# Row maxima of the two widest query blocks: half copied by ScalarE, a VectorE scan over both halves, the causal mask by TensorE, and a new order

## The reference, cut to what matters

```python
x = layernorm(inputs); qkv = (x @ W_qkv + b).reshape(4, 16, 1024, 48)
q, k, v = split(qkv); qk = einsum('bhse,bhte->bhst', q, k) * 512 ** -0.5
attn = softmax(qk + triu(-inf, k=1)); sa = attn @ v; out = sa @ W_out + b_out
# light_ffn(x) and scatter(heavy_ffn(x[top 256 by routing])) are added
```

## Time and profile before

| | |
|---|---|
| time, median of 3 runs (lowest to highest) | 708.96 us (708.54 to 710.82) |
| span of the profiled execution (first to last instruction) | 705.6 us |
| own time of the profiled execution | not listed apart from its span; the median is 3.4 us above the span |
| busy: PE, DVE, ACT, POOL | 660.3, 563.1, 392.4, 380.6 us |
| mean granted TensorE clock | 0.979 |

### The profile page before, as it was taken

How to read it: one execution, slowest core, us unless ns; L and a number is a source line. 1 busy time by engine, 2 the same in 40 slices (tenths; PEclk the granted TensorE clock), 3 DMA queues, 4 the chain that set the end, 5 groups by cost and what they waited for, 6 DMA issues and landing times. The chain is left out here.

```text
span 705.6 us, 12334 instructions
## 1 busy us (share of the span) xinstructions
PE 660.3 (94%) x3923; PEld 291.7 (41%) x3923; DVE 563.1 (80%) x1587; ACT 392.4 (56%) x876; POOL 380.6 (54%) x774
## 2 busy tenths in 40 slices
PE   4995999899999999989999999999999999999995
PEld 2552555333333333323323333333333434678675
DVE  4853888899999999999999999999999595563211
ACT  2331322387877777728858868777776565230210
POOL 4663550358858657657886755554543274431603
PEclk9997999899999999979999999999999999999999
DMA  8675999769786676795999648458484261956512
GB/s 274 195 183 159 230 237 235 173 134 153 136 140 138 90 139 103 97 145 94 164 152 150 122 87 120 74 54 118 79 159 35 42 123 34 207 107 163 106 60 30
DMA packets 259776, 92.48 MB, mean 131 GB/s; under 512 B 229808, under 2 KB 245328, under 8 KB 256592
## 3 DMA queue, kind: packets, MB, share of 16 engines
q1 hardware_dynamic: 258176, 89.60, 65.9%
q0 software_dynamic: 1536, 2.10, 1.7%
HBM read 56.65 MB, written 35.01 MB: 130 GB/s over the span
## 5 line engine op out<-in xcount | busy, mean ns | idle before, releaser
L1268 DVE CUSTOM_DVE_ANT_0 ps<-ps,maskrow 128x640 f32<-128x640 f32 (+7 forms) x512 | 375.3, 779 | 27.6 <-PE ps L1034 26.0
L904 ACT ACTIVATE strips<-ps 128x512 f32<-128x512 f32 (+1 forms) x608 | 313.0, 577 | 111.0 <-PE ps L1076 88.7
L1034 PE MATMUL ps<-QTk,QTq 96*128 96x512 bf16 (+3 forms) x768 | 190.5, 337 | 22.6 <-DVE mx L1268 15.4
L1076 PE MATMUL ps<-QTq,QTk 99*128 99x512 bf16 (+3 forms) x768 | 185.4, 331 | 1.5 <-DMA QTq<-m_d 0.6
L1094 PE MATMUL ps<-strips,vext 128*32 128x512 f32 (+3 forms) x1536 | 162.0, 497 | 0.9 <-DVE oT L1291 0.4
L1034 PEld LDWEIGHTS ps<-QTk,QTq 96*128 96x128 bf16 x768 | 53.7, 98 | 170.9 <-DVE mx L1268 137.2
L1076 PEld LDWEIGHTS ps<-QTq,QTk 99*128 99x128 bf16 x768 | 68.4, 98 | 88.3 <-ACT strips L904 40.2
L1747 POOL TENSOR_SCALAR_AFFINE_SELECT strips<-strips 128x512 f32<-128x512 f32 x128 | 79.4, 636 | 41.6 <-ACT strips L904 41.2
L994 PE MATMUL ps<-shared,xrT 128*128 128x384 f32 (+1 forms) x256 | 94.9, 503 | 0.1
L1268 DVE DVE_READ_ACCUMULATOR2_ANT mx<- 128x1 f32 x512 | 72.3, 141 | 0.0
L1640 POOL TENSOR_TENSOR r<-qkT,pieces 128x1024 f32<-128x1024 f32 x16 | 34.1, 2132 | 50.2 <-ACT pieces L883 41.9
(11 more groups left out here) (154 smaller groups left out, 668.3 us busy)
## 6 DMA issues: line engine op xcount, KB each, us to landing
pieces_d<-pieces SPq DMA_DIRECT2D x64, 192.0 KB, 3.5
qk<-qkv_d SPq DMA_DIRECT2D x64, 128.0 KB, 3.9
qkv_d<-shared SPq DMA_DIRECT2D x16, 384.0 KB, 4.0
QTq<-pieces_d SPq DMA_DIRECT2D x16, 384.0 KB, 5.1
QTk<-pieces_d SPq DMA_DIRECT2D x16, 384.0 KB, 7.6
QTq<-pieces_d SPq DMA_DIRECT2D x16, 256.0 KB, 5.7
QTk<-pieces_d SPq DMA_DIRECT2D x16, 256.0 KB, 8.3
vext<-qkv_d SPq DMA_DIRECT2D x16, 256.0 KB, 5.8
```

What stands on the lines that cost most here:

```text
L904: nc.scalar.activation(dst, src, ACT.Exp, scale=SCALE).then_inc(exp_done, 1)
L1034: mm = pe.matmul(psM[:, s, at:at + n], QTq[0:W, f % 3, c * 1024 + qb * P:c * 1024 + (qb + 1) * P], QTk[0:W, f % 3, c * 1024 + k0:c * 1024 ...
L1076: mm = pe.matmul(psE[:, (NE * q + j) % ES, k * n:(k + 1) * n], QTk[0:W + 3, q % 3, c * 1024 + kb * P:c * 1024 + (kb + 1) * P], QTq[0:W + 3 ...
L1268: ins = nc.vector.tensor_tensor_reduce(scores, scores, maskrow[:, 1024 - n:1024], 1.0, MASKED, ALU.add, ALU.max, mx[:, f % 2, 8 * c + qb:8 ...
```

## The change

Query blocks 7 and 6 (1024 and 896 scores a row) become "paired" items, in steps 2 to 15. For each of them TensorE computes the products as before and then adds the causal mask in PSUM by one more 128 x 128 product (`eye` times `barred`). ScalarE copies the left half of the scores to SBUF (`half_copied`, items "H"; two buffers, laid over `xr` and `osb`). VectorE takes `tensor_tensor_scan` with max and max over the right half in PSUM and the copy in SBUF: element i of its output is the larger of output i-1, right[i] and left[i]. It writes 512 or 448 running maxima to `scan`, placed so that the last lands in the column of `mx` for that block. Since a scan overwrites what lies left of that column, the C items run from head 3 down to head 0, with the narrow blocks of a head behind the scans (`maxima_of`), and each item waits for the scan before it. `mx` is now one buffer and part of `scan`. The blocks 0 to 5 are handled as before.

```diff
-UNITS = ((4,), (5,), (6,), (7,), (0, 1), (2, 3))
+UNITS = ((7,), (6,), (5,), (4,), (2, 3), (0, 1))
+PAIRED = (0, 1)
+def maxima_of(f):
+    return [("C", f) + x for c in range(3, -2, -1) for x in ((c, 0), (c + 1, 4), (c, 1), (c + 1, 5), (c, 2), (c, 3))
+            if 0 <= x[0] < 4]
+NHB = 2
-STEP, PACE = 29.60, 29.94
-SOON, LATER, BEHIND = 0.15, 8.0, 1.44
+STEP, PACE = 23.944, 24.244
+SOON, LATER, BEHIND = 0.150, 11.860, 1.729
...
+            if kind == "H":
+                n = HALVES.index(x) - NHB
+                return latest(after(("Tensor", ("C",) + x[1:])), after(("Vector", ("C",) + HALVES[n][1:] if n >= 0 else ("SMAX",))))
...
-            return ... if engine == "Tensor" else 0.12 + 0.00084 * n
+            return ... if engine == "Tensor" else 0.075 + 0.00082 * n
+        if kind == "H":
+            return 0.075 + 0.00082 * (UNITS[x[3]][0] + 1) * P / 2
+            if x[3] in PAIRED and x[1] > 1:
+                return product_time(widths[0]) + BARRED if engine == "Tensor" else 0.117 + widths[0] / 2 / 960
...
+            def half_copied(f, c, u):
+                s, at = place["C", f, c, u]
+                act.wait_ge(full[s], at + 1)
+                k, n = paired["C", f, c, u], (UNITS[u][0] + 1) * P // 2
+                if k == 1:
+                    act.wait_ge(smax_done, 1)
+                elif k >= NHB:
+                    so, to = place[("C",) + HALVES[k - NHB][1:]]
+                    act.wait_ge(free[so], to + 1)
+                nc.scalar.activation(half[k % NHB][:, 0:n], psM[:, s, 0:n], ACT.Copy).then_inc(half_done, 1)
...
+                            masked = item in paired and k0 + n == (qb + 1) * P
...
+                            if masked:
+                                mm = pe.matmul(psM[:, s, at - P:at], eye[:, :], barred[:, :], start=False, stop=True)
...
+                before = scan_before["C", f, c, u]
+                if before:
+                    so, to = place[before]
+                    dve.wait_ge(free[so], to + 1)
...
+                    if ("C", f, c, u) in paired:
+                        k = paired["C", f, c, u]
+                        dve.wait_ge(half_done, k + 1)
+                        scores = psM[:, s, n // 2:n]
+                        end = MXAT + 8 * c + qb + 1
+                        ins = nc.vector.tensor_tensor_scan(scan[:, end - n // 2:end], scores, half[k % NHB][:, 0:n // 2],
+                                                           MASKED, ALU.max, ALU.max)
+                        continue
```

More of the change, by code:

```diff
@@ L73 @@
 EARLY, BEGUN = 3, 12
-FIRST = [("C", f, c, u) for f in range(2) for c in range(4) for u in range(NU)][:4 * NU + BEGUN]
+def maxima_of(f):
+    return [("C", f) + x for c in range(3, -2, -1) for x in ((c, 0), (c + 1, 4), (c, 1), (c + 1, 5), (c, 2), (c, 3))
+            if 0 <= x[0] < 4]
+FIRST = (maxima_of(0) + maxima_of(1))[:4 * NU + BEGUN]
 NL = 8
+HALVES = [("H",) + x[1:] for x in [x for f in range(1, STEPS) for x in maxima_of(f)][BEGUN:]
+          if x[1] > 1 and x[3] in PAIRED]
+NHB = 2
+MXAT = 504
 LAG = 0.2
-STEP, PACE = 29.60, 29.94
-SOON, LATER, BEHIND = 0.15, 8.0, 1.44
+STEP, PACE = 23.944, 24.244
+SOON, LATER, BEHIND = 0.150, 11.860, 1.729
 OB = 1
@@ L89 @@
 LANDS = 1.6
+BARRED = 0.06
 def product_time(n):
@@ L103, in schedule @@
     chains = {
-        ("Tensor", "C"): [("C", f, c, u) for f in range(1, STEPS) for c in range(4) for u in range(NU)][BEGUN:],
+        ("Tensor", "C"): [x for f in range(1, STEPS) for x in maxima_of(f)][BEGUN:],
         ("Tensor", "E"): [("E", q, j) for q in range(STEPS) for j in range(NE)],
@@ L111, in schedule @@
         ("Scalar", "E"): [("E", q, j) for q in range(STEPS) for j in range(NE)],
+        ("Scalar", "H"): list(HALVES),
         ("Scalar", "R"): [x for r in range(N_ITERS) for x in (("RX", r), ("R", r))],
         ("Vector", "TP"): [("TP", f) for f in range(EARLY, STEPS)],
-        ("Vector", "C"): [("C", f, c, u) for f in range(1, STEPS) for c in range(4) for u in range(NU)][BEGUN:],
+        ("Vector", "C"): [x for f in range(1, STEPS) for x in maxima_of(f)][BEGUN:],
         ("Vector", "MXT"): [("MXT", f) for f in range(1, STEPS)],
@@ L191, in ready @@
             if kind == "KEY":
-                return latest(done.get(("landed", ("NA_IN",))), after(("Vector", ("C", STEPS - 1, 3, NU - 1))))
+                return latest(done.get(("landed", ("NA_IN",))), after(("Vector", ("C", STEPS - 1, 0, NU - 1))))
             if kind == "SMAX":
@@ L197, in ready @@
             if kind == "MXT":
-                return latest(after(("Vector", ("C", x[1], 3, NU - 1))), after(("Pool", ("MAX", x[1] - 1))) if x[1] > 1 else 0.0)
+                return latest(after(("Vector", ("C", x[1], 0, NU - 1))), after(("Pool", ("MAX", x[1] - 1))) if x[1] > 1 else 0.0)
             if kind == "OT":
@@ L207, in ready @@
                 return latest(after(("Pool", ("S", x[1] - 1) if x[1] else ("ROUTES",))), PACE * (0.9 + 0.75 * x[1]))
+            if kind == "C" and x[1] > 2 and x == maxima_of(x[1])[0]:
+                return after(("Scalar", ("H",) + x[1:]), ("Vector", ("MXT", x[1] - 1)))
+            if kind == "C" and x[3] in PAIRED and x[1] > 1:
+                return after(("Scalar", ("H",) + x[1:]))
             return after(("Tensor", x))
         if engine == "Scalar":
+            if kind == "H":
+                n = HALVES.index(x) - NHB
+                return latest(after(("Tensor", ("C",) + x[1:])), after(("Vector", ("C",) + HALVES[n][1:] if n >= 0 else ("SMAX",))))
             if kind == "P1":
@@ L273, in due @@
         if kind == "TP":
-            return STEP * (x[1] - 2.40)
+            return STEP * (x[1] - 2.388)
         if kind == "P1":
-            return STEP * (x[1] - 2.23)
-        if kind == "C":
-            return STEP * (x[1] - 1.61 + (NU * x[2] + x[3]) / (4 * NU))
+            return STEP * (x[1] - 2.218)
+        if kind in ("C", "H"):
+            return STEP * (x[1] - 1.756 + maxima_of(x[1]).index(("C",) + x[1:]) / (4 * NU))
         if kind == "E":
@@ L281, in due @@
         if kind == "PV":
-            return STEP * (x[1] + 0.38 + EXPS_OF[x[2:]] / NE)
+            return STEP * (x[1] + 0.366 + EXPS_OF[x[2:]] / NE)
         if kind == "CAUSAL":
@@ L285, in due @@
         if kind == "SPLIT":
-            return STEP * (x[1] - 2.31)
+            return STEP * (x[1] - 2.298)
         if kind in ("STORE", "LOAD", "LQK"):
-            return STEP * (x[1] - 2.13)
+            return STEP * (x[1] - 2.118)
         if kind == "BULK":
@@ L370, in layer_kernel @@
     order, slots, _ = schedule()
+    paired = {("C",) + x[1:]: n for n, x in enumerate(HALVES)}
     place = {x: (0, n) for n, x in enumerate(FIRST)}
@@ L376, in layer_kernel @@
         place[x] = n % MS, held[n % MS] + n // MS
+    scan_before, last_scan = {}, None
+    for x in [x for f in range(STEPS) for x in maxima_of(f)]:
+        scan_before[x] = last_scan
+        if x in paired:
+            last_scan = x
     ST = 10
@@ L472, in layer_kernel @@
         pmo = sb("pmo", [P, 2, 32, D])
-        mx = sb("mx", [P, 2, 32])
+        scan = sb("scan", [P, MXAT + 32])
+        mx = scan[:, MXAT:MXAT + 32]
+        sT = scan[0:NT, 0:P]
         mxT = sb("mxT", [P, 32])
@@ L520, in layer_kernel @@
                 oT[:, :, :, :].rearrange("p b n w -> p (b n w)")[:, 0:QKV]]
+        half = [xr[:, :, :].rearrange("p u e -> p (u e)"), osb[:, 0:512]]
         xs = strips[:, 0:NT * E].rearrange("p (t e) -> p t e", e=E)
@@ L1024, in ring_item @@
                     _, f, c, u = item
-                    if c == 0 and u == 0:
+                    if c == 3 and u == 0:
                         pe.wait_ge(qk_in[f % 3], 16 * 2 * len(RUNS) * (f // 3 + 1))
@@ L1106, in _ @@
                     project(t // 2, t % 2, h)
+            pe.wait_ge(consts, N_CONST)
             pe.wait_ge(qkv_done, NT)
@@ L1258, in largest @@
                 dve.wait_ge(full[s], at + 1)
-                if c == 0 and u == 0 and f >= 2:
-                    dve.wait_ge(mxt_done, f - 1)
+                if c == 3 and u == 0 and f >= 1:
+                    dve.wait_ge(mxt_done, f)
+                before = scan_before["C", f, c, u]
+                if before:
+                    so, to = place[before]
+                    dve.wait_ge(free[so], to + 1)
                 where = 0
```

30 lines of the change are left out of this document (19 added, 11 removed).

## The result

The changed kernel takes 763.4 us (median of 4 runs, 763.0 to 764.3) against 708.8 us; the ratio is 1.077 with a 95% interval of 1.074 to 1.079. The forecast was 758 us, with 700 to 790 as its range. The profiled execution has a span of 761.8 us.

The account below looks back on a forecast made before the run. VectorE was taken to bound the kernel at 29.5 us a step; a slot round of 33.0 us a step over 14 steps adds 49 us to 705.6, plus 3.4 from span to median: 758 us, range 700 to 790.

Parts of the forecast that it names:

- VectorE bounds the kernel before: From 140 to 555 us VectorE, 96% busy, was taken to set the pace, with 28.3 of 29.5 us a step.
- The mask product: On TensorE, 128 more columns for each paired item: 0.06 us, eight times a step, 0.5 us, in time TensorE has.
- The scan's price: On VectorE, 1.19 us for a scan of 512 and 1.05 for 448, so 9.0 us replace 8.8 a step.
- upper end: The scan at 2.08 ns an element, from GpSimd's subtraction, saving VectorE nothing; the lower end, at the maximum's rate, saves 4.0 us a step.
- The copies: On ScalarE, 0.60 and 0.55 us each, 4.6 us a step; ScalarE at 26.5 of 29.5 us still fits.
- The round of the slot: TensorE writes, ScalarE copies, VectorE reads one slot: 6.70 us of parts plus 1.56 of waits, 8.26 us a head.
- The sum: Steps 2 to 15 at 33.0 us instead of 29.5 add 49 us; 754.6 us of span, 758 us median.
- Rival 1: Scan at the maximum's rate, slot still sets the pace: 28.9 us a step, 701 us (687 to 717); chance 0.13.
- Rival 2: Quick scan, planner's order hides the rounds, ScalarE bounds at 26.5 us a step: 667 us; chance 0.05.
- Rival 3: Slow scan, copy hidden behind the other slot and VectorE's other duties: 29.7 us a step, 712 us; chance 0.13.
- Rival 4: Forecast with a mismatched order, in-order queues waiting for each other, TensorE's clock possibly lost: 785 us and above; chance 0.07.
- Front and tail unchanged: The parts before and after the steps with scans keep their time; the median stands 3.4 us above the span.

## Why the prediction was right, and where it wasn't

- *VectorE bounds the kernel before.* Only half true. VectorE is 96% busy, but TensorE is 97% busy in the same stretch (402.6 of 415 us). With 4 us a step of VectorE's work gone the kernel won 8 us, and 17 with a new plan, and TensorE was busy 386 of 390 us then. My sentence that TensorE "has this time" took its 119.9 us of waits for room. The mask product came out small all the same (3.6 us between the medians), so that this error cost the forecast little.
- *The scan's price.* Forecast 1.19 and 1.05 us from start to next start. Measured: 483.83 to 484.97 us, 1.14, and 485.58 to 486.56, 0.98. The median durations, 1223 and 1090 ns, are 64 elements apart: 2.08 ns an element.

```profile
L1333 DVE TENSOR_TENSOR_SCAN scan<-ps,xr x56: 1160/1223/1225, 152.5 to 598.4; 128x512 f32<-128x512 f32 x56
L1333 DVE TENSOR_TENSOR_SCAN scan<-ps,osb x56: 1027/1090/1092, 154.2 to 601.0; 128x448 f32<-128x448 f32 x56
```
```profile
483.83 1.22 DVE L1333 TENSOR_TENSOR_SCAN scan<-ps,xr 128x512 f32<-128x512 f32 x1 [0.34 <-ACT xr L962]
...
484.97 0.69 DVE L1359 STREAM_TRANSPOSE oT<-ps 128x512 f32<-128x512 f32 x1
...
485.58 1.05 DVE L1333 TENSOR_TENSOR_SCAN scan<-ps,osb 128x448 f32<-128x448 f32 x1
...
486.56 0.22 DVE L1364 RECIPROCAL rden<-oT 128x16 f32<-128x16 f32 x1
```

  The trace now agrees with the Trainium skill (DVE: opcode table, instruction layouts, handler registers and perf-mode slots; Datapath and trigger behaviour), which gives the scan half the throughput: 2.08 ns an element against the 1.0 ns of the maximum. That upper end was chosen by an argument on two dependent operations, and its price was read from a row of GpSimd, another engine. The runs show the rate and not its reason; that GpSimd's 2.08 ns fits to the last digit is luck.
- *The copies.* Forecast 0.60 and 0.55 us, measured 602 and 548 ns.
- *The mask product.* Forecast 0.06 us; 0.07 in the chain. Over 112 of them the forecast was 7 us, and 3.6 us lie between the medians, with overlapping intervals.
- *The round of the slot.* Forecast 2.70 us for the 1024-wide item; the chain shows 0.60 + 0.07 + 0.61 + 0.12 + 1.23, with 0.07 of issue before the write and before the copy, 2.70. VectorE's waits name ScalarE's copy, as said, and its share fell to 86% (forecast 87%). One thing was overlooked: the slots alternate from item to item, and the first head of a step has no narrow pairs in between, so that its 896-wide item falls into the other slot. In the other three heads (42 in the trace) the mean rounds, from TensorE's start in a slot to its next start there, are 2.87, 2.93 and 2.27 us. That is 8.1 us a head, against 6.70 of parts and 1.56 of waits in the forecast.
- *The sum.* 33.0 us a step was forecast, 33.2 measured. How close that came is luck. I put all 49 us on the round and nothing on the order. The runs show some 17 us that stay when scan, copy and mask product are all gone (724.4 us), and 39 us for scan, copy and mask product together. An order priced at nothing and a round priced some 10 us too high made up for each other, if the two parts simply add, which no run shows. The measured round of 8.1 us doesn't tell the two apart, since waits that the order makes fall into it.
- *Rival 1* (701 us with a quick scan, 687 to 717) was measured at 723.7: with a scan at the old rate, copy, mask product and order still lose 17 us. *Rival 2* (667 us) had no ground: even with no copy it is 710.6. *Rival 3* (waits covered, 712 us) was not so; VectorE sat idle 64 of 460 us. *Rival 4* had the 17 us of the order in it, though not 785 us. Its loss of clock didn't happen in the changed kernel (0.98), but did in a replanned one (0.95).
- *Front and tail unchanged.* 2.4 us less and 3.0 us more. The 3.4 us from the span to the median were 1.6.

What stays open is how much of the 17 us belongs to a plan made for a step of 24 us, how much is the chance of its constants, and how much the single buffer of `mx`. The kernel before moved by 14 us with other constants, and for the changed kernel a plan at the true price came with another clock. No version here computes the whole result and beats the kernel before.

## What to carry to other kernels

Before an engine is relieved, take its work away outright and time that: here half of the two widest maxima were worth 8 us, or 17 with the one new plan that was tried, before any price of sharing them. A third engine in the round of a doubly buffered slot brings its own duration into the round: here a copy of 0.6 us, eight times a step, cost 13 us beside a quick reader and 30 beside a slow one. Write the round down link by link before the change. And a halved width is no gain if each element costs twice: look for the price of an element of the new instruction, not for its count.

## What the runs showed of the hardware

- `tensor_tensor_scan` with two maxima on fp32, one input in PSUM and one in SBUF: 1219 ns for 512 pairs and 1076 for 448, on the mean. The fused add and maximum on the same operands takes 697 for 512.
- The granted clock changed with the plan. With the same instructions another plan took it from 0.99 to 0.94 in the main stretch (0.98 and 0.95 to 0.96 over the whole, in four executions each). In the kernel with 0.94, a stretch of 60 us in which TensorE was busy 53.1 us had 0.84, which is between the levels of 1.2 and 2.4 GHz, and one in which it was busy 57.4 us had 1.00, the level of 2.4 GHz:

```profile
200.00:260.00 60.00, 53.09 (x311) 18.47 (x311) 53.37 (x137) 46.49 (x107) 45.70 (x86) 0.84 0.82 132
...
320.00:380.00 60.00, 57.35 (x410) 20.00 (x408) 53.02 (x136) 51.16 (x121) 40.95 (x87) 1.00 0.72 113
```

  The changed kernel in the same two stretches, at 1.00 in both:

```profile
200.00:260.00 60.00, 53.00 (x365) 17.38 (x365) 54.08 (x141) 49.03 (x115) 44.77 (x92) 1.00 0.86 138
...
320.00:380.00 60.00, 52.33 (x362) 17.71 (x355) 55.24 (x142) 46.92 (x111) 47.64 (x96) 1.00 0.70 125
```

  It was busy 53.0 us where the other was busy 53.1 at 0.84, so TensorE's busy time over a stretch doesn't tell its clock.

- A small product with its own weights (128 x 128, 223 ns busy) took 0.07 us in the chain, behind the two products of its item.
